# Moving one of twelve destination one-hots from VectorE to GpSimd in the count phase of a graph-network kernel

## The reference

```python
for i in range(3):
    agg = scatter_logsumexp(h[edge_src], edge_dst, N)
    hc = concatenate([h, agg], -1)
    h_new = relu(layer_norm(hc @ W_l[i].T + b_l[i], gamma_l[i], beta_l[i]))
    h = 0.5 * h + 0.5 * h_new
```

## Time and profile before

| what | us |
|---|---|
| median of 3 runs | 3775.7 (3775.6 to 3780.91) |
| profiled execution, device time | 3775.88 |
| its span, first to last instruction | 3774.1 |
| DVE / PE / ACT / POOL busy in the span | 1652.0 / 2935.2 / 1465.5 / 1648.5 |

### The profile page before, as it was taken

How to read it: one execution, slowest core, us unless ns; L and a number is a source line. 1 busy time by engine, 2 the same in 40 slices (tenths; PEclk the granted TensorE clock), 3 DMA queues, 4 the chain that set the end, 5 groups by cost and what they waited for, 6 DMA issues and landing times.

```text
span 3774.1 us, 59761 instructions
## 1 busy us (share of the span) xinstructions
PE 2935.2 (78%) x17152; PEld 2062.4 (55%) x17152; DVE 1652.0 (44%) x3486; ACT 1465.5 (39%) x2187; POOL 1648.5 (44%) x1721
## 2 busy tenths in 40 slices
PE   0049999999589599468888888888888888888845
PEld 0036777777489499444445545454444454555545
DVE  3159999999810500732222222222222222222227
ACT  6067888888300200123333333333333333333312
POOL 0125000000000000077777777777777777777642
PEclk9999999999799799778887887878888888888756
DMA  2103222222389298146666666666666666666510
GB/s 100 40 13 137 118 105 117 119 119 111 145 319 397 119 390 342 44 120 163 168 164 162 168 164 163 166 159 171 163 161 168 165 164 168 163 164 163 149 45 17
DMA packets 360500, 584.11 MB, mean 155 GB/s; under 512 B 42813, under 2 KB 256060, under 8 KB 341398
## 3 DMA queue, kind: packets, MB, share of 16 engines
q1 hardware_dynamic: 306038, 472.45, 37.2%
q0 software_dynamic: 54432, 111.30, 13.6%
HBM read 394.90 MB, written 191.89 MB: 155 GB/s over the span
## 4 chain that ended last, share of the span: by engine, by line
POOL 29%; PE 28%; issue 16%; DVE 15%; DMA 7%; SPq 3%; DVEq 2%; ACT 1%; POOLq 0%; ACTq 0%
POOL arena L548 27%; PE ps L672 13%; DVE arena L1336 6%; DMA arena<-p_tab,m_idx 6%; PE ps L747 4%; PE ps L689 4%; SPq L339 3%; PE ps L591 2%; PE ps L756 2%; PE ps L744 2%; PE ps L579 1%; POOL ends L521 1%; DVEq L1336 1%; PE ps L764 1%; DVE ends L1035 1%
## 5 line engine op out<-in xcount | busy, mean ns | idle before, releaser
L548 POOL DMA_INDIRECT arena<-p_tab,m_idx x1568 | 1486.4, 948 | 1741.2 <-issue 1708.9
L1409 DVE TENSOR_TENSOR_SCAN arena<-arena,ps 128x512 f32<-128x512 f32 x392 | 501.6, 1280 | 1037.8 <-ACT ps L934 936.8
L747 PEld LDWEIGHTS ps<-ident,arena 128*128 128x128 f32 x3136 | 480.6, 234 | 639.9 <-DMA arena<-p_tab,m_idx 482.3
L747 PE MATMUL ps<-ident,arena 128*128 128x128 f32 x3136 | 571.4, 338 | 296.8 <-DMA arena<-p_tab,m_idx 296.3
L929 ACT ACTIVATE arena<-ps 128x512 f32<-128x512 f32 x392 | 234.0, 597 | 1040.4 <-PE ps L747 1031.9
L672 PE MATMUL ps<-arena 128*128 128x192 bf16 x5635 | 494.6, 247 | 67.0 <-DVE arena L1302 66.0
L756 PE MATMUL ps<-arena,weights 128*128 128x512 f32 x784 | 530.3, 767 | 0.0
L1336 DVE TENSOR_SCALAR arena<-iota_w,arena 128x392 bf16<-128x392 f16 x2156 | 523.1, 324 | 0.0
L672 PEld LDWEIGHTS ps<-arena 128*128 128x128 f16 x5635 | 472.1, 98 | 81.0 <-issue 66.3
L689 PE MATMUL ps<-arena 128*128 128x392 bf16 x2352 | 460.9, 337 | 69.5 <-DVE arena L1336 69.0
L744 PE MATMUL ps<-arena,weights 17*128 17x512 f32 x784 | 486.1, 702 | 0.0
(11 more groups left out here) (193 smaller groups left out, 1870.6 us busy)
## 6 DMA issues: line engine op xcount, KB each, us to landing
arena<-count_d SPq DMA_DIRECT2D x66, 1568.0 KB, 8.3
arena<-keep_d SPq DMA_DIRECT2D x392, 256.0 KB, 4.4
scan_rows<-arena SPq DMA_DIRECT2D x392, 256.0 KB
count_d<-arena SPq DMA_DIRECT2D x49, 1568.0 KB
wide<-count_d SPq DMA_DIRECT2D x32, 1568.0 KB, 8.2
arena<-p_tab,m_idx POOLq DMA_INDIRECT x1568
arena<-attr_in SPq DMA_DIRECT2D x392, 34.0 KB
p_tab<-wide SPq DMA_DIRECT2D x7, 448.0 KB, 3.0
```

Of the source, the lines that this page charges most:

```text
L548: pool.indirect_dma_start(m_rows[:, k, t, :], None, p_tab, bass.IndirectOffsetOnAxis(ap=m_idx[:, k, t:t + 1].bitcast(U32), axis=0))\
L747: last = pe.matmul(x[:, t * P:(t + 1) * P], m_rows[:, k, t, :], ident[:, :], start=False, stop=(t == TB - 1), skip_group_check=True)
L1409: dve.tensor_tensor_scan(m_scan[:, k % SCAN_RING, :], m_mask[:, k, :], m_term[k % TERM_RING], before, ALU.mult, ALU.add).then_inc(e1.scan_ ...
```

## The change

GpSimd gets one destination one-hot of each quad, `hot_a[:, 3, 1, :]`; VectorE builds 10, ScalarE keeps its one. At the start of every block GpSimd copies the block's 16 keys into `pool_keys`. For quad n it waits until all windows of the quads before have been counted, then builds its one-hot. TensorE waits for it before the fourth window of the quad. The new code stands behind the reading of `use_counts` on GpSimd.

```diff
-DVE_HOTS = QUAD - 1
+DVE_HOTS = QUAD - 2
...
+        pool_keys = sb("pool_keys", [P, WB])
...
             counts = pool.to_reg(pool.value_load(use_counts[0:1, 0:1], min_val=0, max_val=1))
+            with pool.If_ne(counts, 0):
+
+                def block_keys(j):
+                    pool.tensor_copy(pool_keys[:, :], keyT_a[:, WT - 2, bass.ds(WB * j, WB)]).then_inc(pool_keys_ready, 1)
+                    pool.wait_ge(pool_keys_ready, j + 1)
+                    pool.sem_inc(alone["pool"], 1)
+
+                def one_hot(q):
+                    w = WSLOTS * q + WSLOTS - 1
+                    pool.tensor_scalar(hot_a[:, WSLOTS - 1, WT - 2, :], iota_w[:, :], pool_keys[:, w:w + 1], None, ALU.is_equal)\
+                        .then_inc(pool_hot_ready, 1)
+
+                pool.wait_ge(keys_copied, 4 * WT)
+                block_keys(0)
+                one_hot(0)
+                for q in range(1, QUADS):
+                    pool.wait_ge(win_counted, WSLOTS * (q + 1))
+                    one_hot(q)
+                with pool.Fori(1, J) as j:
+                    pool.wait_ge(win_counted, WSLOTS * (QUADS * j + 1))
+                    block_keys(j)
+                    for q in range(QUADS):
+                        pool.wait_ge(win_counted, WSLOTS * (QUADS * j + q + 1))
+                        pool.sem_inc(alone["pool"], 1)
+                        one_hot(q)
             with pool.If_eq(counts, 0):
...
                         if s == WSLOTS - 1:
+                            pe.wait_ge(pool_hot_ready, QUADS * j + q + 1)
                             pe.wait_ge(act_hot_ready, QUADS * j + q + 1)
```

More of the change, by code:

```diff
@@ L241, in build @@
             "hot_ready", "win_counted", "block_part", "block_free", "bank_free"))
-        src_hot_ready, act_hot_ready, square_ready = (sem(n) for n in ("src_hot_ready", "act_hot_ready", "square_ready"))
+        src_hot_ready, act_hot_ready, square_ready, pool_hot_ready = (sem(n) for n in (
+            "src_hot_ready", "act_hot_ready", "square_ready", "pool_hot_ready"))
+        pool_keys_ready = sem("pool_keys_ready")
         block_stored = [sem(f"block_stored{r}") for r in range(2)]
```

## The result

The changed kernel takes 3897.79 us (median of 4 runs, 3892.04 to 3912.59), the kernel before 3778.3 us beside it (4 runs, 3775.6 to 3780.91). The ratio is 1.0322, with a 95% interval of 1.029 to 1.0355: **slower by 3.2%**. The profiled execution took 3893.2 us, with a span of 3891.4, against 3774.1 before: 117.3 us more.

What follows compares the result with a forecast made beforehand. The prediction took VectorE to bound the count phase. From 3775.7 us it added 60 (late start), 1 (clock), 53 (net hold-up) and 7 (key copies) to reach 3897 us, with a range of 3788 to 4030.

Steps and rivals of the forecast that it cites:

- The first one-hot comes late: Count phase start: GpSimd's one-hot follows its 49 fetches, so the fourth window starts at 347.5 instead of 287.3, +60 us.
- +1 for the clock: Count phase start: TensorE, cold after the stall, resumes at half clock for two quads, +1 us.
- +81: Count phase start: other end of the late-start delay, if the fetches land after 23.3 us instead of 2.5.
- the 366.4: Count phase start: time in us when the last fetch has landed, if landing takes 23.3 us; 345.6 with 2.5.
- VectorE is held up 0.50 us a quad: Count phase, each quad: VectorE loses GpSimd's 0.60 us less 0.10 us of overlap between one-hots, so 0.50 us.
- A net +0.27 us a quad: Count phase, 196 quads: 0.50 us of hold-up against 0.231 us saved on VectorE, +53 us in all.
- The copy of the keys: Each block's start: GpSimd's copy, 49 times about 0.15 us, adds +7 us if VectorE is held up, otherwise nothing.
- So all 45 us would count: Count phase: one one-hot less a quad leaves VectorE 13.0 us a block against TensorE's 12.44, gaining 45 us.
- no hold-up: Rival, count phase: GpSimd's short one-hot slips between VectorE's; 3792 us in all, chance 0.17.
- Starvation: Rival, count phase: GpSimd gets in only when VectorE stands; quads of 4.41 us, 4025 us in all, chance 0.14.
- Faster: Rival, count phase: fetches go much faster while VectorE stands, no hold-up after; 3771 or 3731 us, chance 0.07 including near it.
- Where `node_ends` would start: End of the count phase: `node_ends` starts near 1088 us instead of 967, shifting all behind it.

Runs made afterwards that it cites:

- e6: Kernel before, with TensorE's fourth window waiting for a GpSimd signal given after its fetches, GpSimd building nothing: 3857.95 us against 3783.11, ratio 1.0158.
- e1: Changed kernel with GpSimd's fetches issued two a block behind its one-hots of blocks 1 to 25: 3832.6 us against 3783.11, ratio 1.0115.
- e2: Kernel before with ten one-hots on VectorE, the eleventh left out, none on GpSimd: 3764.26 us against 3783.11, ratio 0.9957.
- e7: Kernel before with ten VectorE one-hots, the eleventh left out, and sums spread over four quads: 4392.53 us against 4420.33, ratio 0.9934.
- e3: Kernel before plus one unread GpSimd tensor_scalar a quad, one input, 392 elements: 3864.96 us against 3783.11, ratio 1.0212.
- e9: Changed kernel with fetches moved behind GpSimd's first one-hots and sums spread over four quads: 3841.84 us against 3776.13, ratio 1.0151.
- e4: Kernel before plus one unread GpSimd tensor_scalar a quad, one input, 196 elements: 4451.19 us (one run) against 4420.33.
- e10: Kernel before plus one unread GpSimd tensor_tensor a quad, two inputs of 392 elements: 3925.13 us (one run) against 3776.13.
- e5: Kernel before plus one unread GpSimd memset a quad, writing 392 elements and reading nothing: 4411.89 us (one run) against 4420.33.

## Why the prediction was right, and where it was not

The total, 3897 us, was met, with a measured median of 3897.79. That it is this close is partly chance: the count phase came 10 us below its terms (111.1 against 121), and the stretches that the change doesn't touch came 6.2 us above the trace before (-12.5 + 16.9 + 1.8); the rest is the spread between runs.

- **The first one-hot comes late: +60 us, and +1 for the clock.** Right, with its chain. The last fetch starts 330.4 - 270.0 = 60.4 us after the first, at 1.26 us each; it lands in 2.5 us, the value taken and not 23.3; TensorE is idle 60.92 us at a granted clock of 0.50. e6 measured the step by itself: 59.7. No run separates the +1. The reason given for 2.5, that VectorE now stands, was wrong: 20.2 to 23.3 us never belonged to these fetches, which land within about 3 us before the change too. The "+81", the 366.4 and the 21 us for a late landing had no ground.
- **VectorE is held up 0.50 us a quad.** The number is right (0.498 in the trace), its derivation is not. I took GpSimd's length as 0.60 us, with bounds of 0.50 and 1.04, and let VectorE lose all but 0.10 of it. GpSimd's one-hot takes 1.28 us alone, outside both bounds, and 2.32 with its wait for the source one-hots; VectorE loses 0.50 of it, on two one-hots of 0.56 us and not one of 0.8. A price too low by half and a share too high by twice cancelled, which is luck. The prediction called itself wrong "if GpSimd's price is outside 0.5 to 1.0 us", and at 1.28 it is: the total held, this part of the mechanism did not. The Trainium skill, page "GPSIMD Engine Reference", section "Elementwise — side-by-side cycle accounting", has the same low price as its best case, an estimate of 0.59 us; the 1.28 measured are more than twice that.
- **A net +0.27 us a quad, +53 us.** Right: the quad went from 3.41 to 3.68 us, and the phase without the late start gained 111.1 - 59.7 = 51.4 (e1: 52.9). Here the saved 0.231 us counts in full, because held up VectorE is above TensorE in every quad.
- **The copy of the keys, +7 us.** Not seen. 51.4 is below the 53 without it, and the block of 14.97 leaves it no room (4 x 3.68 + 0.27 = 14.99).
- **"So all 45 us would count": this step failed.** I compared 13.0 us of VectorE with 12.44 us of TensorE over a whole block. The two meet every quad, and in three of four TensorE already needed 3.42 to 3.50 us. e2 measured 14.7 us; e7 shows that 32.5 can be had once the quads are even. The error did not reach the forecast, since the hold-up kept VectorE the longer engine, but it did reach the rivals: "no hold-up" would have been 3775.7 + 61 - 15 = 3822 us and not 3792, and with the first one-hot in time the gain would have been 15 us and not 45.
- **The rivals.** No hold-up: refuted by the block of 14.97 us and by e3. Starvation: refuted, since the block is not 17.6 and TensorE waits for VectorE alone. GpSimd's operation waits about 1 us for the source one-hots and then gets in among the destination one-hots. The late landings that spoke for this rival were a misreading, as told above. (e3's fetches, told below, were kept out by VectorE for over 5 us; the one-hots never met that.) Faster: refuted by the pace of the fetches (1.26 us each) and by e1 and e9, which have no late start and lose all the same.
- **Where `node_ends` would start.** Predicted 1088, found 1065.8: 12.5 of the 22 us are the shorter setup, 10 the count phase.

What stays open: why a one-input operation stretches two one-hots of VectorE and a two-input one a single one, and why GpSimd gives way to the source one-hots (two inputs themselves) even where it began first; only once each in e4 and e10 was it the source one-hots that were stretched (1.14 and 1.59 us). No experiment separated these. Open too are what a write costs beside destination one-hots, and the regime of e3's fetches, told below. No run was made in which the one-hot goes to GpSimd in pieces.

## What to carry to other kernels

Work that is given to an engine comes behind all that this engine has queued, so ask first when it will have the first piece ready: 49 fetches that nobody needed yet made half of this loss. Slack between two engines that hand over a single buffer has to be reckoned per handover, as the sum of the longer ones, and not per block. Work handed to GpSimd beside a saturated VectorE must save more there than it costs there: here it saved 0.231 us a quad and cost 0.50.

## What was not expected of the hardware

- GpSimd's `tensor_scalar` of 392 elements takes 1.28 us alone, longer than its `tensor_tensor` of the same length, 0.87 us (the shortest in e10, with VectorE at work), yet the latter costs VectorE more (0.59 against 0.44 us a quad in e3).
- GpSimd's operations wait for VectorE's source one-hots if they read (after, e3, e10), and mostly wait for them to begin if they only write (e5).
- The same 49 fetches land about equally soon whatever VectorE does: within about 3 us for the last of them before, 2.5 us (median) where VectorE stands (after, e6), and 2.6 us where VectorE works and two come a block (e1).
- In e3 the fetches, with the code in front of them unchanged, lasted until 412.7 us instead of 347.9 and took up to 8.18 us each. GpSimd and VectorE in that stretch, merged from two timelines of e3:

```profile
342.37 6.53 POOL L503 DMA_INDIRECT wide<-dst_in,end_idx  x1 [0.30 <-issue]
348.68 0.96 DVE L1334 TENSOR_TENSOR arena<-iota_s,arena 128x1536 bf16<-128x1536 bf16 x1
349.20 3.11 POOL L503 DMA_INDIRECT wide<-dst_in,end_idx  x1 [0.30 <-issue]
352.10 0.96 DVE L1334 TENSOR_TENSOR arena<-iota_s,arena 128x1536 bf16<-128x1536 bf16 x1
```

  Both fetches end 0.2 us after source one-hots have begun (348.90 and 352.31), as if VectorE's run of destination one-hots had kept GpSimd out and the source one-hots had let it in. VectorE lost nothing. It is the pattern of e5's memsets. In the other executions in which the fetches follow one another they take 0.94 to 0.95 us (median) beside the same one-hots, single ones up to 3.79 (e10); what decides between the two is open. GpSimd's operations of e3 began 64 us later for it (at 419 instead of some 355 us), and the first of them caught up one behind the other.
- At the same granted clock of 1.00 and busy all the time, TensorE did 46 matmuls in 10 us of the setup in one execution and 83 in another.
